# Batch 0 normalized by halves with a root on ScalarE, the exponential's table loaded behind it, and batch 1's statistics moved back, in a gated attention block

## What is computed

```python
xn = layernorm(x)                                   # per token, eps 1e-5
q, k, v = split(xn @ Wqkv + bqkv)                   # s = attention + gated FFN of xn
qp, kp = elu(q) + 1, elu(k) + 1
attn = (qp @ (kp.T @ v)) / (qp @ kp.sum(tokens) + 1e-6)
x1 = layer_norm(xn + attn, g1, b1)
s = layer_norm(x1 + (silu(x1 @ Wg + bg) * (x1 @ Wu + bu)) @ Wd + bd, g2, b2)
gf = global_net(xn.mean(tokens))                    # 3 small layers, per batch
for _ in range(3):                                  # o starts as xn
    o = o + coupling(gf, coupling_net(o)) * twist(o)
out = x + s * silu(o)
```

## Time and profile before

| | |
|---|---|
| time, median of 3 runs | 168.56 us (168.51 to 168.80) |
| time of the profiled execution | 168.63 us |
| its span in the trace | 166.8 us |
| busy: PE, DVE, ACT, POOL | 153.5, 139.8, 125.1, 109.4 us |

### The profile page before, as it was taken

How to read it: one execution, slowest core, us unless ns; L and a number is a source line. 1 busy time by engine, 2 the same in 40 slices (tenths; PEclk the granted TensorE clock), 3 DMA queues, 4 the chain that set the end, 5 groups by cost and what they waited for, 6 DMA issues and landing times.

```text
span 166.8 us, 3383 instructions
## 1 busy us (share of the span) xinstructions
PE 153.5 (92%) x932; PEld 118.0 (71%) x932; DVE 139.8 (84%) x551; ACT 125.1 (75%) x319; POOL 109.4 (66%) x206
## 2 busy tenths in 40 slices
PE   5979999999999999999999999999999999999700
PEld 5657989889988786454545545788888888888700
DVE  2897699899988988599999969878698988967864
ACT  3669786999999988888887876994778687364230
POOL 0386776798973689990022175399978869679980
PEclk9999999999999999999999999999999999999995
DMA  5895222021120000000000000000001101011013
GB/s 179 257 384 133 63 65 63 0 65 37 32 63 0 2 6 0 0 0 0 4 0 0 6 0 2 0 0 4 0 2 63 63 4 65 0 63 65 4 63 126
DMA packets 11923, 7.84 MB, mean 47 GB/s; under 512 B 8960, under 2 KB 9728, under 8 KB 11904
## 3 DMA queue, kind: packets, MB, share of 16 engines
q1 hardware_dynamic: 11616, 7.55, 15.0%
q10 hardware_dynamic: 288, 0.08, 0.2%
HBM read 3.43 MB, written 2.10 MB: 33 GB/s over the span
## 4 chain that ended last, share of the span: by engine, by line
PE 55%; DVE 24%; ACT 8%; POOL 6%; issue 5%; DVEq 0%; ACTq 0%; POOLq 0%
PE bank L1135 10%; PE bank L1124 6%; PE bank L1125 6%; PE bank L1126 6%; DVE r_tok L684 5%; DVE pq L698 5%; PE bank L948 5%; DVE r_tok L687 4%; PE bank L1014 3%; PE bank L1060 2%; PE bank L1025 2%; PE bank L1005 2%; PE bank L1003 2%; PE bank L1004 2%; PE bank L965 2%
## 5 line engine op out<-in xcount | busy, mean ns | idle before, releaser
L472 ACT ACTIVATE pq<-bank,bffn 128x512 f32<-128x512 f32 (+1 forms) x24 | 16.4, 686 | 13.6 <-PE bank L1126 13.4
L259 POOL TENSOR_TENSOR rstd<-ve,minus_half 128x4 f32<-128x4 f32 (+1 forms) x25 | 24.7, 987 | 2.1
L1135 PEld LDWEIGHTS bank<-wd,pq 128*128 128x128 f32 x168 | 20.9, 191 | 1.4
L1135 PE MATMUL bank<-wd,pq 128*128 128x128 f32 x168 | 21.0, 274 | 0.0
L739 DVE SCALAR_TENSOR_TENSOR pq<-bank,bffn,pq 128x512 f32<-128x512 f32 (+1 forms) x24 | 17.5, 738 | 3.6 <-PE bank L1126 2.6
L1124 PE MATMUL bank<-x_hi,ffn_hi 128*128 128x512 f32 (+1 forms) x48 | 20.2, 421 | 0.0
L1125 PE MATMUL bank<-x_lo,ffn_hi 128*128 128x512 f32 (+1 forms) x48 | 18.9, 393 | 0.0
L1126 PE MATMUL bank<-x_hi,ffn_lo 128*128 128x512 f32 (+1 forms) x48 | 18.8, 392 | 0.0
L423 ACT ACTIVATE q_stage<-bank,col 128x512 f32<-128x512 f32 x24 | 16.3, 687 | 2.6 <-PE bank L948 1.5
L257 POOL TENSOR_SCALAR nm<-mv 128x4 f32<-128x4 f32 x23 | 5.1, 223 | 17.7 <-DVE mv L581 17.4
L1003 PE MATMUL bank<-first_hi,xT_hi 128*128 128x512 f32 x32 | 14.4, 451 | 0.0
(11 more groups left out here) (150 smaller groups left out, 437.0 us busy)
## 6 DMA issues: line engine op xcount, KB each, us to landing
x_tok<-in_x SPq DMA_DIRECT2D x8, 256.0 KB, 6.5
tx_tok<-xn_tok SPq DMA_DIRECT2D x16, 128.0 KB, 2.5
out<-pq SPq DMA_DIRECT2D x7, 256.0 KB, 2.0
r_tok<-in_w_ffn SPq DMA_DIRECT2D x1, 341.0 KB, 6.8
r_tok<-in_w_first SPq DMA_DIRECT2D x1, 320.0 KB, 3.5
out<-pq SPq DMA_DIRECT2D x2, 128.0 KB, 1.8
row<-in_rows SPq DMA_DIRECT2D x1, 192.0 KB, 6.4
wd<-in_w_down SPq DMA_DIRECT2D x1, 192.0 KB, 6.8
```

Of the source, the lines that this page charges most:

```text
L259: return pool.tensor_tensor(rstd[i][:, b, ts], ve[i][:, b, ts], minus_half[:, ts], ALU.pow)
L472: act.activation(sg[n % 2][0:m], gate_of(n)[0:m], ACT.Silu, bias=bffn[0:m, c:c + 1]).then_inc(sg_ready, 1)
L1135: last = pe.matmul(dst[:, t * P:(t + 1) * P], hid[b % 2][0:m, c, t * P:(t + 1) * P], wd[0:m, c], start=(c == 0), stop=(c == CHUNKS - 1))
```

## The change

On **ACT** the first table loaded is that of the square root, and behind the first bias diagonal ACT takes the root of batch 0's variance plus eps (`std0`). The exponential's table is loaded behind the last diagonal. The high part of the transposed batch 0 is made in two halves of 256 columns (`hi_first`), between the copy of q's weights and that of the others. On **DVE** the constant for the warm-up is set first; batch 0's negated mean and the reciprocal of `std0` are computed and batch 0 normalized right behind its statistics; batch 1's statistics follow; the low part is made in two halves (`lo_first`), ahead of the low part of the other weights; and at batch 7 the two halves' sums are first added (`sums`). **POOL** no longer computes batch 0's reciprocal root. **PE** starts its warm-up as soon as its operand is set, with eight matmuls, transposes batch 0 into two banks and signals each half, and in each k, v projection multiplies by the low part of the weights last.

```diff
-WARM = 7
+WARM = 8
...
+        ps_xT0 = [bank[0][:, 0:2 * P], bank67[:, 2]]
...
 # POOL
             pool.tensor_scalar(bias_col[:], col[:, 0:2], 1.0, 1.0, ALU.mult, ALU.add).then_inc(shifted_ready, 1)
-            power(0, 0).then_inc(rstd0_ready, 1)
             norm_x(1)
...
 # ACT
+            def hi_first(half):
+                act.wait_ge(xT0_ps, half + 1)
+                act.activation(xT_hi[:, 0, 2 * P * half:2 * P * (half + 1)], ps_xT0[half], ACT.Identity,
+                               bias=offset[:, 0:1], accum_out=half_sums[:, half, 0:1]).then_inc(xT0_hi_ready, 1)
...
-            act.activation(spare[:], minus_one[:], ACT.Exp)
+            act.activation(spare[:], offset[:], ACT.Sqrt)
...
             act.mul(bias_diag[:, D:2 * D], eye, col[:, COL["bv"]:COL["bv"] + 1])
+            act.wait_ge(mv_ready[0], 1)
+            act.activation(std0[:], mv[0][:, 0, :, 1], ACT.Sqrt, bias=eps[:, 0:1]).then_inc(std0_ready, 1)
             act.wait_ge(shifted_ready, 1)
             act.mul(bias_diag[:, 0:D], eye, bias_col[:, 1:2])
             act.mul(bias_diag[:, 3 * D:4 * D], eye, bias_col[:, 0:1]).then_inc(diag_ready, 1)
+            act.wait_ge(std0_ready, 1)
+            act.activation(spare[:], minus_one[:], ACT.Exp)
             act.wait_ge(w_ps, 1)
             act.copy(first_hi[:, 4 * D:5 * D], ps_wq).then_inc(first_hi_ready, 1)
+            hi_first(0)
+            hi_first(1)
             act.wait_ge(w_ps, 2)
             act.copy(first_hi[:, 0:4 * D], ps_w[:]).then_inc(first_hi_ready, 1)
-            hi_x(0)
...
 # DVE
             def norm_first(b):
+                dve.wait_ge(std0_ready, 1)
+                dve.reciprocal(rstd[0][:, b], std0[:]).then_inc(rstd0_ready, 1)
                 dve.wait_ge(rstd0_ready, 1)
+                dve.wait_ge(nm0_ready, 1)
...
+            def lo_first(half):
+                dve.wait_ge(xT0_hi_ready, half + 1)
+                cs = slice(2 * P * half, 2 * P * (half + 1))
+                ins = dve.scalar_tensor_tensor(out=xT_lo[:, 0, cs], in0=ps_xT0[half], scalar=offset[:, 0:1],
+                                               in1=xT_hi[:, 0, cs].bitcast(F32), op0=ALU.add, op1=ALU.subtract,
+                                               accum_out=half_sums[:, half, 1:2])
+                if half:
+                    ins.then_inc(xT_lo_ready, 1)
...
+            dve.memset(spread, 1.0 / (D * OFFSET)).then_inc(warm_ready, 1)
...
             stats_x(0)
+            dve.wait_ge(mv_ready[0], 1)
+            dve.tensor_scalar(nm[0][:, 0], mv[0][:, 0, :, 0], -1.0, None, ALU.mult).then_inc(nm0_ready, 1)
+            norm_first(0)
             dve.wait_ge(x_loaded[1], 16)
             measure(0, 1, x_tok[:, 1])
-            norm_first(0)
+            moments(0, 1)
             dve.wait_ge(first_hi_ready, 1)
             dve.tensor_tensor(first_lo[:, 4 * D:5 * D], ps_wq, first_hi[:, 4 * D:5 * D].bitcast(F32),
                               ALU.subtract).then_inc(first_ready, 1)
-            moments(0, 1)
+            lo_first(0)
+            lo_first(1)
             dve.wait_ge(first_hi_ready, 2)
             dve.tensor_tensor(first_lo[:, 0:4 * D], ps_w[:], first_hi[:, 0:4 * D].bitcast(F32),
                               ALU.subtract).then_inc(first_ready, 1)
-            lo_x(0)
             bias_rows()
...
                 if b == BATCHES - 1:
+                    dve.tensor_tensor(sums[:, :, 0], half_sums[:, 0], half_sums[:, 1], ALU.add).then_inc(sums_ready, 1)
+                    dve.wait_ge(sums_ready, 1)
                     dve.wait_ge(xT_lo_ready, BATCHES)
...
 # PE
-                    last = pe.transpose(ps_xT[:, t * P:(t + 1) * P], xn_tok[:, 0, t], eye)
-                last.then_inc(xT_ps, 1)
+                    last = pe.transpose(ps_xT0[t // 2][:, t % 2 * P:(t % 2 + 1) * P], xn_tok[:, 0, t], eye)
+                    if t in (1, 3):
+                        last.then_inc(xT0_ps, 1)
...
                 pe.matmul(dst[:], hi, first_hi[:, 0:4 * D], start=True, stop=False)
-                pe.matmul(dst[:], hi, first_lo[:, 0:4 * D], start=False, stop=False)
-                pe.matmul(dst[:], lo, first_hi[:, 0:4 * D], start=False, stop=True).then_inc(k_ps, 1)
+                pe.matmul(dst[:], lo, first_hi[:, 0:4 * D], start=False, stop=False)
+                if n == 0:
+                    pe.wait_ge(first_ready, 2)
+                pe.matmul(dst[:], hi, first_lo[:, 0:4 * D], start=False, stop=True).then_inc(k_ps, 1)
...
+            pe.wait_ge(warm_ready, 1)
+            warm_up(WARM)
             pe.wait_ge(consts_ready, 1)
-            warm_up(WARM)
```

More of the change, by code:

```diff
@@ L79, in gated_block @@
         sign = sb("sign", [P, 1])
-        spare = sb("spare", [P, 1])
+        spare, eps = sb("spare", [P, 1]), sb("eps", [P, 1])
+        std0 = sb("std0", [P, TILES])
         offset, minus_mean, minus_mean_sign = sb("offset", [P, 1]), sb("minus_mean", [P, 1]), sb("minus_mean_sign", [P, 1])
@@ L141, in gated_block @@
         rden = sb("rden", [P, BATCHES, TILES])
-        sum_hi, sum_lo, ctx_sum = sb("sum_hi", [P, BATCHES]), sb("sum_lo", [P, BATCHES]), sb("ctx_sum", [P, BATCHES])
+        sums, ctx_sum = sb("sums", [P, 2, BATCHES]), sb("ctx_sum", [P, BATCHES])
+        sum_hi, sum_lo = sums[:, 0], sums[:, 1]
+        half_sums = sb("half_sums", [P, 2, 2])
         gh1, gh2, gt = sb("gh1", [P, BATCHES]), sb("gh2", [P, BATCHES]), sb("gt", [P, BATCHES])
@@ L177, in gated_block @@
         ffn_hi_ready, pool_const, cols_ready, consts_ready = sem("ffn_hi_ready"), sem("pool_const"), sem("cols_ready"), sem("consts_ready")
+        warm_ready, nm0_ready, xT0_ps, xT0_hi_ready, sums_ready, std0_ready = [
+            sem(n) for n in ("warm_ready", "nm0_ready", "xT0_ps", "xT0_hi_ready", "sums_ready", "std0_ready")]
         centre_ready, shifted_ready, diag_ready, w_ps, rstd0_ready = [
@@ L370, in hi_x @@
             def hi_x(b):
-                act.wait_ge(xT_ps, b + 1)
+                act.wait_ge(xT_ps, b)
                 if b >= 2:
@@ L602, in norm_first @@
                                       rstd[0][:, b, t:t + 1], ALU.add, ALU.mult).then_inc(xn0_ready, 1)
+            def lo_first(half):
[6 more added lines that the diff above has]
+                    ins.then_inc(xT_lo_ready, 1)
             def lo_x(b):
-                dve.wait_ge(xT_hi_ready, b + 1)
+                dve.wait_ge(xT_hi_ready, b)
                 if b >= 2:
@@ L817, in _ @@
             dve.memset(offset[:], OFFSET)
+            dve.memset(eps[:], LN_EPS)
             dve.memset(minus_mean[:], -1.0 / D)
-            dve.memset(spread, 1.0 / (D * OFFSET))
             dve.memset(bias_diag[:, 2 * D:3 * D], 0.0)
@@ L853, in _ @@
                 if b == BATCHES - 1:
+                    dve.tensor_tensor(sums[:, :, 0], half_sums[:, 0], half_sums[:, 1], ALU.add).then_inc(sums_ready, 1)
+                    dve.wait_ge(sums_ready, 1)
                     dve.wait_ge(xT_lo_ready, BATCHES)
-                    dve.scalar_tensor_tensor(out=ctx_sum[:], in0=sum_hi[:], scalar=-OFFSET * SEQ, in1=sum_lo[:],
+                    dve.scalar_tensor_tensor(out=ctx_sum[:], in0=sum_hi, scalar=-OFFSET * SEQ, in1=sum_lo,
                                              op0=ALU.add, op1=ALU.add).then_inc(ctx_ready, 1)
@@ L981, in project_q @@
             def project_q(b):
-                pe.wait_ge(xT_hi_ready, b + 1)
                 if b == 0:
+                    pe.wait_ge(xT0_hi_ready, 2)
                     pe.wait_ge(first_ready, 1)
+                else:
+                    pe.wait_ge(xT_hi_ready, b)
                 if b >= 1:
@@ L997, in project_tokens @@
                 if n == 0:
-                    pe.wait_ge(first_ready, 2)
+                    pe.wait_ge(first_hi_ready, 2)
                 if n >= 3:
```

## The result

The changed kernel took 169.29 us (median of 19 runs, 168.87 to 170.21), the kernel before 168.69 us (19 runs, 168.46 to 169.39) in the same sessions. The ratio is 1.0031, with a 95% interval of 1.0020 to 1.0042: 0.3% slower, where 0.2% was forecast. The medians lie 0.60 us apart, where 0.33 was forecast. Its profiled execution took 168.97 us, 0.34 more than that of before.

A forecast was written before the change was run, and what follows sets the result against it. Bound: in the first 10 us the chain of waits over PE, ACT and DVE, with DVE's queue from 9.87 to 12.06 as second bound. Sum: 168.63 − 0.05 + 0.38 = 168.96 us profiled, 168.89 against the median; range 168.1 to 169.3.

The forecast's parts named there:

- Prologue, chain: First 10 us, root to q's last matmul: that matmul starts at 9.29 instead of 10.00, 0.71 us earlier.
- Prologue, what is kept: At `feature_q(0)`: DVE's queue swallows 0.66 us of the gain; it starts at 11.38, the prologue is worth 0.05 us.
- the bound of 0.15 more: Prologue's error bound: up to 0.15 us more gained, or as much lost, from short activations and high-part halves.
- One sign of the forecast: End of the prologue: `sum_kv(0)` would start within 0.1 of 12.40 if the forecast was right.
- Rival C: Prologue: the 0.71 us arrive in full, giving 168.18 us, or 167.85 without batch 7's loss; chance 12%.
- Batch 7: At batch 7: POOL's work holds the added 128x2 sum, then the 128x8 sum; `copy_kv(6)` starts 0.38 us later.
- Rival F: ACT's prologue table load has to wait for a drain: priced at +1.28 us, 170.2 us; chance 3%.
- Rival E: Prologue: PE stays at the low clock, moving the chain back by 1.5 us, about 170.4 us; chance 4%.
- Further on there is no event with a time of its own on the chain, so a shift in front reaches the end whole.: Behind the prologue: nothing on the chain has its own time, so an earlier shift reaches the end whole.
- Rival D: Batch 7: all three POOL negations hold the 128x8 sum, 1.13 us instead of 0.38, 169.64 us; chance 7%.
- Sum: Whole kernel: 168.63 profiled − 0.05 + 0.38 = 168.96 us, or 168.89 against the median, 0.2% slower.
- the main case: Whole kernel: case A, prologue and batch 7 as forecast, 168.6 to 169.1 us; chance 62%.

The follow-up runs named there:

- run 3: Changed kernel with batch 2's statistics moved behind `feature_k(0)`: 168.60 us, 0.9990 of the kernel before.
- run 4: Changed kernel with batch 7's two sums moved behind `feature_k(30)` and batch 2's statistics behind `feature_k(0)`: 168.01 us, 0.9961 of the kernel before.
- run 5: Kernel before with batch 2's statistics moved behind `feature_k(0)`: 168.69 us, ratio 0.9992.
- run 1: Kernel before plus only a 128x2 sum of zeros at batch 7, for which the 128x8 sum waits: 169.34 us, ratio 1.0049.
- run 2: Changed kernel with both sums of batch 7 moved behind `feature_k(30)`, where POOL is idle: 168.74 us, 1.0010 of the kernel before.
- experiment 9: Kernel before with batch 2's statistics moved behind `feature_k(0)` and batch 7's sum behind `feature_k(30)`: 168.24 us, ratio 0.9977.
- Run 8: Changed kernel with the old warm-up of seven matmuls, from about 1.7 us on: 169.50 us, 1.0032 of the kernel before.
- run 6: Kernel before with its one 128x8 sum of batch 7 moved behind `feature_k(30)`: 168.34 us, ratio 0.9961.
- run 10: Kernel of run 4 with POOL's product `scale_x1(5)` put ahead of `norm_x1(6)`: 168.03 us, 0.9963 of the kernel before.
- run 11: Kernel before with only POOL's product `scale_x1(5)` put ahead of `norm_x1(6)`: 168.51 us, ratio 0.9982.
- run 12: Kernel of run 4 with the small tiles `eps` and `std0` declared behind the large ones: 168.00 us, 0.9958 of the kernel before.

## Why the prediction was nearly right

- **Prologue, chain.** Right, and the start was lucky. The root at 5.13 (forecast 5.22), table load 6.01 to 7.30 (6.08 to 7.36), copy of the weights to 9.07 (9.20), last q matmul at 9.22 (9.29). The low half took 0.46 on the chain, not 0.42. From the root to the q matmul it is 4.09 us, 4.07 forecast. The gain of 0.78 us instead of the forecast 0.71 comes from the input, which landed 0.17 earlier; without that it would have been an estimated 0.6.
- **Prologue, what is kept.** Right in kind, small in size: `feature_q(0)` at 11.27 (forecast 11.38), worth 0.16 to 0.22 us, not 0.05, at the edge of the bound of 0.15 more. Most of that miss is the input again: 0.78 less 0.17 (input) and 0.56 (statistics) leaves an estimated 0.05, as forecast. One sign of the forecast failed by this: `sum_kv(0)` came at 12.17, not within 0.1 of 12.40. The reason is shown by runs 3, 4 and 5 and by the table of experiment 4: with the statistics out of the way the gain arrives, and without the change moving them gives nothing. Rival C did not come.
- **Batch 7.** Right: 0.39 seen, 0.38 forecast; shown by the traces of runs 1 and 2, and without the prologue by `feature_k(0)` to `copy_kv(7)` (0.41 for the change, 0.37 for run 1). The medians bear it out only roughly: run 1 lost more than 0.38. The Trainium skill's rule ("SBUF — State Buffer", "Who interferes with whom") holds for the tensor_tensor too, 0.60 to 0.63 us beside POOL and 0.15 alone.
- **Rival F.** The load starts 0.02 us after the last diagonal (6.00 to 6.01) and costs its 1.28 us; the 1380 ns of drain that the Trainium skill ("ScalarE: Activation LUTs", "What ACT_TABLE_LOAD costs") gives are not seen here.
- **Rival E.** The rate rose in all traces, at 4.0 to 7.2 us, so a late rise is no rare accident: it comes in executions with either prologue. In profiled executions `feature_k(0)` starts between 11.79 and 12.44 in the kernel before and its variants, between 11.10 and 11.99 in the changed ones with the statistics late, 11.99 being the one with the rise at 7.2. The price of 1.5 us was for a rise that never comes, and no trace has that. What a late rise did cost was put at nothing. The changed prologue loses 0.56 us to the statistics however late the rise is, but with a rise at 6.7 us or later it wins only 0.3 at the q matmul (experiment 9). By that estimate it is 0.25 us slower than the old one in such an execution; no trace shows the changed kernel itself in that case.
- **"Further on there is no event with a time of its own on the chain, so a shift in front reaches the end whole."** This failed. `coupling(0)` at 69 us takes 0.34 to 0.99 us, by how POOL's instructions happen to lie, and what reaches slot 1 moves with it by up to 0.5. Rival D, the 128x8 sum passed over at batch 7, did not come: wherever it stands there, it took its turn at the first chance. But what D describes did happen at `coupling(0)`, in 6 of 14 traces.
- **Sum.** In the profiled pair −0.22 (prologue), +0.41 (batch 7), +0.04 (`coupling(0)`), +0.01 (the couplings), +0.10 (FFN, tiles moved by 20 bytes) make the 0.34 seen at the end. That the profiled time met the forecast to 0.01 us (168.97, 168.96) is luck: the prologue gave 0.17 more than forecast, batch 7 took 0.03 more, and the terms that the forecast did not have took 0.15. The median of 169.29 lies above the main case (168.6 to 169.1) and 0.01 inside the range, partly because the kernel before was itself 0.13 slower in these sessions than the 168.56 that the forecast starts from. Rival C's price counts 0.05 us twice; it should read 168.23, not 168.18.
- **What stays open.** Of the 0.60 between the medians 0.26 are not explained. There are two candidates. One is executions in which DVE is passed over at `coupling(0)`; the other is executions in which PE's rate rises late. Run 8's profiled execution of 169.44 us has both: against that of the changed kernel it is 0.25 us late at `copy_kv(6)`, with the rise at about 6.1 us, and loses 0.24 more at `coupling(0)`. Unprofiled executions don't show which of the two they had.

## What to carry to other kernels

When a prologue's chain is shortened, look first at what the next consumer's own engine has queued: 0.56 of 0.78 us were lost to statistics that nobody needed yet, and moving them is worth it only together with the change. Before trusting one profiled execution, compare when its input landed and when PE's rate rose: here these moved the prologue by as much as the change did. A distance between two events on the path (q matmul to `feature_k(0)`) is free of both. A tiny VectorE instruction with two SBUF inputs costs what GpSimd happens to be running; put it where GpSimd idles (0.15 us in place of 0.6; the kernels of runs 2 and 6 took about 0.5 us less). Declare new small tiles behind the large ones, so that a comparison isn't muddied by moved operands.

## What the runs showed of the hardware

- While POOL's instructions follow each other without a pause, DVE's held `coupling(0)` is let in between two of them in 8 traces (0.34 to 0.64 us) and passed over once in 6 (0.84 to 0.99). What decides is open. A one-input tensor_scalar of POOL holds it too (0.84 us in run 10, 0.44 in run 11), and in those two runs a tensor_scalar of DVE, `base`, took 1.01 us and ended with POOL's product beside it; it takes 0.30 in run 4.
- PE's rate doubled at 4.0 to 7.2 us, also between kernels whose programs are the same up to there (4.0 in run 4, 7.2 in run 3), while the granted clock reads 1.00 from 0 to 12 us in the traces of the kernel before, the changed one and run 3.
- With the large tiles moved by 20 bytes in SBUF, the FFN's fp32r matmuls start 1 to 5 ns further apart, some 0.3 us over all 144 of them; with the small tiles declared last (run 12) most of that goes. Why is open.
